# A 32-head attention inside a four-layer kernel: the eight-bit weights' mask and rounding four and three heads later, one large load in four parts

## The reference, cut to what matters

```python
# layer 2, mixer: 32 heads of 8 numbers over 256 keys per batch
logits = jnp.einsum('bqhd,bkhd->bhqk', q, k) * scale
w = jax.nn.softmax(logits, axis=-1)
attn = jnp.einsum('bhqk,bkhd->bqhd', w, v).reshape(b, n, 256)
return attn @ Wout + bout
...
# layer 2, feed-forward: weights rounded to eight bits
wq = w.astype(jnp.float8_e4m3fn).astype(x.dtype)
y = jnp.einsum('bsi,io->bso', x, wq) * scale
...
# layer 3, feed-forward: 16 experts of width 176, the best 2 for each token, and a shared one
y = y + _swiglu(t, w1[e], w3[e], w2[e]) * w_e[:, None]
```

## Time and profile before

| what | value |
|---|---|
| runs shown | 1047.06, 1041.70, 1039.58 us; median 1041.7 |
| the profiled execution | 1044.17 us, its span 1042.4 us |
| TensorE clock granted, mean over the span | 0.869 of full speed |
| PE busy | 839.0 us, 80% of the span |
| DVE busy | 698.1 us, 67% |
| POOL busy | 417.0 us, 40% |
| ACT busy | 390.9 us, 37% |

### The profile page before, as it was taken

How to read it: one execution, slowest core, us unless ns; L and a number is a source line. 1 busy time by engine, 2 the same in 40 slices (tenths; PEclk the granted TensorE clock), 3 DMA queues, 4 the chain that set the end, 5 groups by cost and what they waited for, 6 DMA issues and landing times.

```text
span 1042.4 us, 12920 instructions
## 1 busy us (share of the span) xinstructions
PE 839.0 (80%) x4202; PEld 528.8 (51%) x4202; DVE 698.1 (67%) x1136; ACT 390.9 (37%) x824; POOL 417.0 (40%) x295
## 2 busy tenths in 40 slices
PE   5887898850688899888489887999884886979993
PEld 2332333340566777677377544555543675645661
DVE  5995999979788889888766554667845546412222
ACT  1433222340334444443255542465550531103331
POOL 4005666400466666666239602333520242232331
PEclk8985888975799999999789896899997996889997
DMA  5102212763022221221020011314126001051114
GB/s 206 45 1 108 74 60 81 282 219 88 0 81 81 81 81 43 78 80 40 0 72 1 31 61 40 119 33 134 34 65 221 12 1 61 22 189 64 46 49 149
DMA packets 28099, 81.67 MB, mean 78 GB/s; under 512 B 3313, under 2 KB 17153, under 8 KB 26529
## 3 DMA queue, kind: packets, MB, share of 16 engines
q1 hardware_dynamic: 25648, 73.25, 20.7%
q0 software_dynamic: 2256, 6.18, 1.7%
q10 hardware_dynamic: 144, 1.57, 0.4%
HBM read 65.64 MB, written 17.35 MB: 80 GB/s over the span
## 4 chain that ended last, share of the span: by engine, by line
PE 47%; DVE 18%; issue 15%; POOL 11%; DMA 3%; ACT 3%; SPq 1%; DVEq 0%; POOLq 0%; ACTq 0%
PE ps L511 6%; POOL M L674 4%; PE ps L1686 4%; PE ps L1327 4%; PE ps L1690 3%; PE ps L390 3%; PE ps L504 3%; PE ps L1728 3%; PE ps L894 2%; DVE M L643 2%; POOL ZT L977 2%; PE ps L1346 2%; DVE M L651 2%; POOL slot_scratch L1212 1%; PE ps L1604 1%
## 5 line engine op out<-in xcount | busy, mean ns | idle before, releaser
L782 PE MATMUL ps<-W,F 128*128 128x256 f32 x544 | 152.3, 406 | 54.4 <-POOL F L737 33.0
L782 PEld LDWEIGHTS ps<-W,F 128*128 128x128 f32 x544 | 103.2, 199 | 86.6 <-DVE W L850 39.5
L585 POOL TENSOR_TENSOR M<-M 128x1024 f32<-128x1024 f32 x32 | 75.2, 2352 | 100.6 <-DVE M L465 53.6
L681 POOL TENSOR_TENSOR W<-W,M 128x1024 f32<-128x1024 f32 x32 | 75.4, 2356 | 84.5 <-DVE M L651 84.5
L1757 ACT ACTIVATE N<-ps 128x512 f32<-128x512 f32 x128 | 69.5, 595 | 86.6 <-PE ps L1690 86.6
L814 ACT ACTIVATE F<-ps 128x128 f32<-128x128 f32 x136 | 37.7, 277 | 149.7 <-PE ps L782 149.6
L643 DVE TENSOR_TENSOR_SCAN M<-ps,M 128x512 f32<-128x512 f32 x64 | 78.0, 1219 | 21.4 <-POOL M L674 21.4
L1686 PE MATMUL ps<-M,W 32*128 32x256 f32 x512 | 78.8, 443 | 16.3 <-DVE W L1784 11.1
L1778 DVE TENSOR_REDUCE W<-ps 128x4 f32<-128x1024 f32 x64 | 78.1, 1221 | 12.5 <-PE ps L1690 9.2
L769 PE MATMUL ps<-W,F 128*128 128x256 f32 x272 | 83.8, 391 | 0.0
L1690 PE MATMUL ps<-W,M 32*128 32x256 f32 x512 | 83.8, 424 | 0.0
(11 more groups left out here) (279 smaller groups left out, 1723.8 us busy)
## 6 DMA issues: line engine op xcount, KB each, us to landing
M<-dbl_scratch SPq DMA_DIRECT2D x48, 512.0 KB, 4.0
W<-in_gu SPq DMA_DIRECT2D x1, 4800.0 KB, 16.2
W<-in_gu SPq DMA_DIRECT2D x1, 4352.0 KB, 14.4
att_scratch<-W SPq DMA_DIRECT2D x32, 128.0 KB
slot_scratch<-in_slots SPq DMA_DIRECT2D x1, 3999.0 KB, 18.7
M<-slot_scratch SPq DMA_DIRECT2D x3, 1032.0 KB, 9.4
W<-in_gu SPq DMA_DIRECT2D x2, 1536.0 KB, 6.9
W<-in_dn SPq DMA_DIRECT2D x1, 2176.0 KB, 19.1
```

The lines of the kernel that those rows point to most:

```text
L585: nc.gpsimd.tensor_tensor(dBu[:, t, :], du[0][:, t, :], Bb[:, par, :], ALU.mult).then_inc(S("dBu_rdy"), 1)
L681: nc.gpsimd.tensor_tensor(u[1][:, t, :], u[1][:, t, :], hC[:, t, :], ALU.add).then_inc(S("y1_acc"), 1)
L782: last = nc.tensor.matmul(up, ztt[:, par, c, :], gu[:, c, s, :], start=(c == 0), stop=(c == DC - 1))
```

## The change

- DVE's mask of the down weights moves from after head 3's maxima to after head 7's.
- POOL's six rounding instructions move from heads 6 to 11 to heads 9 to 14. The numbers 0 to 5 that they are given stay the same.
- `dn3a` is loaded in four parts of four experts each (512 KB), after the stores of heads 2, 4, 6 and 8; `dn3s` after the store of head 10. `LD_W3` goes from seven loads to ten.
- The other four loads after the store of head 0 stay.

```diff
--- before.py
+++ after.py
@@ -59,7 +59,7 @@
 ROW = DIM + 2
 RING = 4
 SLOT_LOADS = (2, 5, 8, 8, 8)
-LD_W3 = 7 * 16
+LD_W3 = 10 * 16
 ZTT_STEPS = [2 * v for v in TILED_STEPS]
 ZTT_BASE = [NT * sum(ZTT_STEPS[:k]) for k in range(4)]
 UNIT_BASE = [sum(NT * f["units"] * v for f, v in zip(FFN[:k], TILED_STEPS)) for k in range(5)]
@@ -1640,7 +1640,10 @@
                     sp.dma_start(dn_scale, a["dns2"].to_broadcast([P, DIM])).then_inc(S("ld_f2_down"), 16)
                     sp.dma_start(wq3, a["wq3"]).then_inc(S("ld_a3"), 16)
                     sp.dma_start(wk3, a["wk3"]).then_inc(S("ld_a3"), 16)
-                    sp.dma_start(dn3a, a["dn3a"]).then_inc(S("ld_w3"), 16)
+                if 2 <= e < 10 and e % 2 == 0:
+                    part = slice((e - 2) // 2 * (NEXP // 4), e // 2 * (NEXP // 4))
+                    sp.dma_start(dn3a[:, part], a["dn3a"][:, part]).then_inc(S("ld_w3"), 16)
+                if e == 10:
                     sp.dma_start(dn3s, a["dn3s"]).then_inc(S("ld_w3"), 16)
                 if e == 12:
                     sp.wait_ge(S("qmax_rdy"), 12)
@@ -1672,8 +1675,8 @@
                 take_values(e)
                 if e == 3:
                     nc.gpsimd.tensor_tensor(X[:], X[:], ob, ALU.add).then_inc(S("x_biased"), 1)
-                if 6 <= e < 12:
-                    fp8_gpsimd(pool, e - 6)
+                if 9 <= e < 15:
+                    fp8_gpsimd(pool, e - 9)
                 if 19 <= e < 31:
                     fp8_gpsimd(pool, e - 13)
 
@@ -1790,7 +1793,7 @@
                 if h < HEADS:
                     maxima(h, 0)
                     maxima(h, 1)
-                if h == 3:
+                if h == 7:
                     fp8_vector(dve, 1)
                 if h == 18:
                     fp8_vector(dve, 0)
```

## The result

| | before | after |
|---|---|---|
| median of 7 runs each, in turn | 1039.66 us | 1032.82 us |
| span of the profiled execution | 1042.4 us | 1030.6 us |
| granted clock, mean | 0.869 | 0.877 |

The ratio after to before is 0.9927, 95% interval 0.9901 to 0.9952: faster by 0.73%, some 7.6 us. (The ratio is that of the means; the medians lie 6.8 us apart.) The forecast ratio was 0.9925, the forecast time 1033.9 us.

A forecast was written before the change was run, and what follows sets the result against it. It took the kernel as mostly a PE-DVE relay, with both engines waiting at head 3 for the scales' load. Terms 5.43 + 2.37 = 7.80 us, other costs 0, from the 1041.7 us median gave 1033.9 us; range 1029 to 1041.

The forecast's parts named there:

- 5.43 us at head 3: Attention loop, head 3: with the mask gone, DVE's query addition starts at 647.80 in place of 653.23, 5.43 us gone.
- 2.37 us at head 4: Head 4: without PE's pause the clock stays full, so it takes 3.94 us, not 6.31; bounds 0 to 2.37.
- The mask at head 7 costs nothing: After head 7's maxima: scales already landed, mask fits DVE's idle 0.95 us; cost 0, upper bound 0.63 us.
- POOL's six instructions: Heads 9 to 14: rounding still ends 14 us before DVE needs it at head 18; cost 0, upper bound 1.8 us.
- SP's issues: SP's queue in the loop: three more issues, 1.3 us altogether, all beside waiting; cost 0.
- the parts: 512 KB load parts behind stores: even a delayed store lands in 8.4 us, needed after 11.8; cost 0, at most a few tenths.
- What follows the loop passes the gain on: After the loop: last stores, gather and layer-3 loads are issued relative to its end, so the gain passes on whole.
- The sum: Whole kernel: 5.43 + 2.37 = 7.80 us gained, 1033.9 us from the median, ratio 0.9925.
- landing beyond 647.80: Head 3: the scales' load delays the mask's start to 652.36, 4.56 us after the addition could start at 647.80.
- The rival on POOL's bias: Head 3: bias holds DVE's query addition to 651.10, costing 3.30 us; gain 4.50, 1037.2 us; chance 8%.

The follow-up runs named there:

- the filled pause: Kernel before, with added matmuls on PE ahead of its wait for head 3's addition: seven gave ratio 0.9998, five 1040.53 us in one run.
- the new pause at head 7: Changed kernel with POOL's bias moved from head 3 to head 7, beside the mask's new place: ratio to before 0.9980.
- the undivided load: Kernel before with only the mask and the rounding moved, the 2 MB load left whole after head 0's store: ratio to before 0.9928.
- the kernel with the separate semaphore: Kernel before, mask kept at head 3, with the scales on a semaphore of their own, waited for only where used: ratio to before 0.9981.
- a half mask: From the changed kernel with head 18's mask halved over heads 18 and 19, and reciprocals cut to 128 columns: ratio to before 0.9887.

## Why the prediction was right

- **5.43 us at head 3.** Forecast: head 3's addition 5.25 us after head 2's (647.80 - 642.55). Measured 5.25.
- **2.37 us at head 4.** Forecast 3.94, measured 3.94. The cause given (the clock fell in PE's pause) held in both tests, the filled pause and the new pause at head 7. The size is that of one profile: the head behind a pause took 5.16 to 6.31 us in the four that have one, so it may be as small as 1.2 in other executions; no run here shows that.
- **The mask at head 7 costs nothing.** Right: 3.94 us, the mask inside the idle 0.95, no wait for the scales. The chosen 0 was the right end of 0 to 0.63.
- **POOL's six instructions, SP's issues, the parts: nothing.** Right; the undivided load gives the same loop to 0.12 us.
- **What follows the loop passes the gain on.** Right to 0.8 us in one profile. Over the eleven profiles the stretch from the last addition to the end took 270.6 to 273.9 us, so a loss of that size can't be told from chance.
- **The sum.** 7.80 us forecast, 7.78 measured in the loop, 0.9925 against 0.9927 in the runs. The spans differed by 4 us more, through an unrelated stage. That the runs agree with the forecast to 0.0002 is luck: their interval is 0.0025 to either side.

One step was wrong though nothing in the sum hung on it. It divided the 5.43 us into 4.56 us of "landing beyond 647.80" and 0.87 us of mask, and said of what is late next only that it is PE's transpose. That holds for a head without the mask. With the mask kept and the landing gone, POOL's bias is late next, by almost as much (head 3 at 9.37 in place of 10.68). The rival on POOL's bias looked at the wrong instruction: it asked whether the bias holds the addition (it doesn't), and not whether it holds the mask. That is why I expected the kernel with the separate semaphore to give 7.8 us, and it gave 2.3 us of loop, of which 1.3 at head 3 and 1.0 at head 4, where the clock was back sooner (PE went on at 652.81 and the window from 656 to 657 us stands at 0.74; in the kernel before it went on at 653.71 and the window with 0.89 begins at 659). Had the change been that one, the forecast would have been wrong by 5.5 us.

## What to carry to other kernels

An idle time is put down to the cause that ends last; before a wait is priced, look for whatever else is running there that would hold the instruction once the wait is gone. In a loop bound by a relay between two engines, work put between costs its excess over the idle time of the engine that runs it, here 0.95 us a head, and nothing else, provided it doesn't meet a GpSimd instruction while it uses the fast form or two SBUF operands. And a pause of PE can cost more than itself: here 3.9 to 5.4 us of pause made the head behind it 1.2 to 2.4 us longer, at half clock.

## What the runs showed of the hardware that I had not expected

- A VectorE mask of 0.96 us took 5.25 and 5.10 us when a GpSimd addition of 4.51 us had started 0.07 and 0.22 us earlier, ending 0.81 us after it both times.
- Beside a GpSimd instruction with one SBUF operand (L1492, 709.42 to 712.19) a half mask took 1.54 us and ended at 711.05, before GpSimd did. So there the second one did not wait for the whole of the first, other than the Trainium skill's rule says. The changed kernel agrees: a product with both operands in SBUF began 1.87 us after the same instruction, 0.90 us before its recorded end, and took no longer than elsewhere (the two lines stand below). GpSimd's spans in a profile are rough: either this instruction holds the others for less than its recorded span, or its recorded end is late, and these traces don't tell which.
- The profiles of the kernel before and of the changed one, the same program up to there, stood 4.8 us apart at the start of the attention, through the input's landing and clock edges in the first mixer; sizes like the ones here can be read from a stage's own length and hardly from spans.

POOL and DVE in the changed kernel, from their timelines:

```profile
717.39 2.77 POOL L1492 TENSOR_SCALAR M<-M 128x768 f32<-128x768 f32 x1
```

```profile
719.26 0.42 DVE L1808 TENSOR_TENSOR ZT<-M 128x256 f32<-128x256 f32 x1
```
